# Second attention: scores of two heads to a block of 64 keys, in two TensorE tiles of 64 rows

## What is computed

```python
b, t1, _ = x.shape
q = x @ Wq + bq
kv = memory @ Wkv + bkv
k, v = jnp.split(kv, 2, axis=-1)
...
q_h = q_h * DK ** (-0.5)
scores = jnp.einsum('bhqd,bhkd->bhqk', q_h, k_h)
mask0 = memory_mask[:, None, :, :] == 0
scores = jnp.where(mask0, -jnp.inf, scores)
attn = jax.nn.softmax(scores, axis=-1)
attn = jnp.where(mask0, 0.0, attn)
ctx = jnp.einsum('bhqk,bhkd->bhqd', attn, v_h)
ctx = ctx.transpose(0, 2, 1, 3).reshape(b, t1, H * DK)
return ctx @ Wout + bout
```

## Time and profile before

| | us |
|---|---|
| median of 3 runs | 2684.61 |
| lowest, highest | 2684.14, 2685.75 |
| profiled execution | 2688.99 |
| its span in the trace | 2687.0 |
| TensorE busy | 2390.7 (89%) |
| VectorE busy | 1575.9 (59%) |
| ScalarE busy | 1234.0 (46%) |
| GpSimd busy | 696.5 (26%) |
| mean granted TensorE clock | 0.978 |

### The profile page before, as it was taken

One profiled execution on the slowest core, in us unless ns is written; L12 is line 12 of the kernel. 1 busy time (PEld: TensorE's weight loads), 2 busy tenths in 40 slices (PEclk: granted clock), 3 DMA queues, 4 the chain that ended last, 5 costly groups with the idle time before them and its releaser, 6 DMA issues.

```text
span 2687.0 us, 37065 instructions
## 1 busy us (share of the span) xinstructions
PE 2390.7 (89%) x13032; PEld 1320.1 (49%) x13032; DVE 1575.9 (59%) x3089; ACT 1234.0 (46%) x2842; POOL 696.5 (26%) x1001
## 2 busy tenths in 40 slices
PE   8889999988888999898888999998888899998776
PEld 3655444445465544354546554454555655444343
DVE  4664624468676561557867555065786746525687
ACT  5753211268584412128858331213876823121485
POOL 0002321037301232013720213102570021310265
PEclk9999999999999999999999999989999999999988
DMA  8001100010300200000030101101003010100000
GB/s 291 17 10 64 33 16 32 0 48 9 110 16 10 70 28 21 27 16 32 9 124 2 57 23 28 39 9 48 1 16 116 2 56 23 44 0 1 1 1 32
DMA packets 58988, 99.43 MB, mean 37 GB/s; under 512 B 13364, under 2 KB 13748, under 8 KB 58296
## 3 DMA queue, kind: packets, MB, share of 16 engines
q1 hardware_dynamic: 58808, 97.06, 10.8%
HBM read 88.66 MB, written 8.39 MB: 36 GB/s over the span
## 4 chain that ended last, share of the span: by engine, by line
PE 63%; ACT 15%; DVE 11%; issue 7%; POOL 3%; DMA 0%; ACTq 0%; DVEq 0%; POOLq 0%; SPq 0%
PE psum L379 21%; PE psum L373 17%; ACT prob L779 6%; PE psum L457 3%; PE psum L523 2%; PE psum L473 2%; ACT xT L808 2%; POOL f_y L362 2%; ACT f_a L966 2%; PE psum L760 1%; DVE f_top L1356 1%; PE psum L665 1%; PE psum L543 1%; PE psum L732 1%; PE psum L594 1%
## 5 line engine op out<-in xcount | busy, mean ns | idle before, releaser
L373 PE MATMUL psum<-xT,weights 128*128 128x512 f32 x1152 | 508.5, 596 | 19.1 <-DMA weights<-in_a_k 10.4
L373 PEld LDWEIGHTS psum<-xT,weights 128*128 128x128 f32 x1152 | 215.1, 191 | 271.5 <-issue 253.2
L379 PE MATMUL psum<-weights,mixed 128*128 128x512 f32 x768 | 337.3, 595 | 3.1 <-DVE mixed L1302 3.1
L1067 DVE TENSOR_REDUCE neg_max<-psum 128x1 f32<-128x128 f32 (+3 forms) x512 | 217.6, 483 | 136.6 <-PE psum L466 71.2
L379 PE MATMUL psum<-weights,xT 128*128 128x512 f32 x640 | 288.9, 596 | 2.4 <-DVE recip L1259 1.6
L1394 POOL TENSOR_SCALAR var<-stats 128x1 f32<-128x1 f32 x192 | 61.7, 321 | 796.3 <-DVE stats L1012 796.3
L779 ACT ACTIVATE prob<-psum,neg_max 128x128 f32<-128x128 f32 (+3 forms) x512 | 263.1, 542 | 4.5 <-DVE neg_max L1067 4.4
L1407 POOL TENSOR_TENSOR f_a<-f_a,f_z 128x256 f32<-128x256 f32 x256 | 193.0, 759 | 166.9 <-DVE f_a L1074 163.9
L379 PEld LDWEIGHTS psum<-weights,mixed 128*128 128x128 f32 x768 | 143.4, 190 | 179.9 <-issue 173.3
L1042 DVE TENSOR_TENSOR x<-psum,x 128x512 f32<-128x512 f32 x128 | 88.4, 690 | 223.4 <-PE psum L379 161.4
L1074 DVE SCALAR_TENSOR_TENSOR f_a<-f_g,conv_w,f_a 128x256 f32<-128x256 f32 x256 | 173.1, 676 | 52.3 <-ACT f_a L966 51.6
(11 more groups left out here) (242 smaller groups left out, 4063.3 us busy)
## 6 DMA issues: line engine op xcount, KB each, us to landing
xT<-in_xT SPq DMA_DIRECT2D x8, 1024.0 KB, 6.6
x<-in_x SPq DMA_DIRECT2D x8, 1024.0 KB, 8.3
out<-x SPq DMA_DIRECT2D x16, 512.0 KB, 2.8
weights<-in_a_k SPq DMA_DIRECT2D x4, 1024.0 KB, 5.0
weights<-in_a_q SPq DMA_DIRECT2D x4, 1024.0 KB, 5.0
weights<-in_a_v SPq DMA_DIRECT2D x4, 1024.0 KB, 5.3
w1f<-in_w SPq DMA_DIRECT2D x4, 1024.0 KB, 14.8
w2f<-in_w SPq DMA_DIRECT2D x4, 1024.0 KB, 17.4
```

Of the source, the lines that this page charges most:

```text
L373: last = mm(bank[:, 0:n], weights[weight][:, c, heads(g)], rhs(c), start=(c == 0), stop=(c == C - 1))
L379: last = mm(bank, lhsT(c), weights[weight][:, c, :], start=(c == 0), stop=(stop and c == C - 1))
L1067: last = v.tensor_reduce(sb["neg_max"][:, n, qc, j:j + 1], bank[:, o:o + P * (qc + 1)], AX.X, ALU.max, negate=True)
```

## The change

A token tile's 16 heads are now scored in one step, in two banks. The step of the first half (`half == 0`) claims two banks, puts the mask in both, and for each chunk `g` runs two products side by side: the partitions 0 to 63 (heads 4g and 4g + 1) into the first bank, the partitions 64 to 127 (heads 4g + 2 and 4g + 3) into the second. Each has 64 rows of contraction and 128 columns, two heads of 64 keys. The step of the second half issues nothing on TensorE but its waits. `b_k` keeps 2 x 64 columns a chunk instead of 4 x 64, and a half now holds two heads of every chunk instead of four heads of two chunks; so the copy to `b_turned` and the sum to `b_sum` write the same elements in another order.

```diff
@@ TensorE, b_score
-                    bank = dve_ring.claim(pe, step)
-                    mm(bank, sb["row_ones"][:], sb["b_mask_row"][:], start=True, stop=False)
-                    for i in range(2):
-                        last = mm(bank[:, 256 * i:256 * i + 256], sb["b_q"][:, 2 * half + i, w * D + P * t:w * D + P * t + P],
-                                  sb["b_k"][:, 2 * half + i, :], start=False, stop=(i == 1))
-                    last.then_inc(dve_ring.filled, 1)
+                    if half == 0:
+                        pair = [dve_ring.claim(pe, ("b_score", w, t, a)) for a in range(2)]
+                        for bank in pair:
+                            mm(bank, sb["row_ones"][:], sb["b_mask_row"][:], start=True, stop=False)
+                        for g in range(C):
+                            for a, bank in enumerate(pair):
+                                r = slice(2 * HD * a, 2 * HD * a + 2 * HD)
+                                last = mm(bank[:, heads(g)], sb["b_q"][r, g, w * D + P * t:w * D + P * t + P],
+                                          sb["b_k"][r, g, :], start=False, stop=(g == C - 1))
+                                if g == C - 1:
+                                    last.then_inc(dve_ring.filled, 1)
@@ ScalarE, b_context
-                            last = run(sb["b_k"][r, g, SK * j:SK * j + SK], bank[r, 0:SK], ACT.Identity,
+                            last = run(sb["b_k"][r, g, SK * (j % 2):SK * (j % 2) + SK], bank[r, 0:SK], ACT.Identity,
                                        bias=sb["b_bias"][r, C + g:C + g + 1])
@@ ScalarE, b_turn
-                    copy(sb["b_turned"][:, w, 4 * half:4 * half + 4, heads(t)],
+                    copy(sb["b_turned"][:, w].rearrange("p (g a) n -> p g a n", a=2)[:, :, half, heads(t)],
                          act_ring.take(act, step).rearrange("p (k n) -> p k n", k=4)).then_inc(act_ring.freed, 1)
@@ VectorE, b_turn
-                    v.tensor_reduce(sb["b_sum"][:, 2 * half:2 * half + 2, t, :],
-                                    sb["b_prob"][:, i % HALF_SLOTS, :].rearrange("p (g j k) -> p g j k", g=2, j=G),
+                    v.tensor_reduce(sb["b_sum"][:, :, t, 2 * half:2 * half + 2],
+                                    sb["b_prob"][:, i % HALF_SLOTS, :].rearrange("p (g j k) -> p g j k", g=C, j=2),
                                     AX.X, ALU.add).then_inc(q["b_summed"], 1)
@@ place
-    again(room, room2, ("b_k", [C, G * SK]), ("b_v", [2 * C, 64]), ("b_q", [C, S]), ("b_prob", [HALF_SLOTS, D]),
+    again(room, room2, ("b_k", [C, 2 * SK]), ("b_v", [2 * C, 64]), ("b_q", [C, S]), ("b_prob", [HALF_SLOTS, D]),
```

## The result

The changed kernel takes 2689.19 us (median of 20 runs, 2687.52 to 2692.3), the kernel before 2685.02 in the runs beside it (20 runs, 2683.84 to 2686.63). Ratio 1.0016, interval 1.0009 to 1.0023: 4.2 us slower, where 7.6 faster was forecast. It lies above the forecast range of 2670 to 2687.5. The profiled execution took 2689.32 (span 2687.3). That is only 0.3 us more span than the kernel before has in its profile (2687.0), whose execution lay 4 us above its median; so whole runs are compared by medians here, and the profiles are used for single stages.

The account below looks back on a forecast made before the run. TensorE was taken as most of the chain of waits, with VectorE setting the pace in places. From 2689.0 us profiled, 6.0 for the stage and 1.6 for the clock gave 2681.4, or 2677.0 off the median; range 2670 to 2687.5.

Parts of the forecast that it names:

- The score step, 1.66: Token tile's whole score step on TensorE: 1.66 us instead of 2.16, saving 0.50 eight times an element.
- The rival that the tiles do not run side by side: Score step's two 64-row tiles do not overlap: 2.46 us instead of 1.66, whole kernel at 2701 us; chance 9%.
- The new wait of 1.7 at the start: Stage start: the second pair waits for VectorE to free a bank, so TensorE stands 1.7 us.
- Then TensorE is again the late one: Behind the start wait TensorE sets the pace: fifth pair done at 924.35, first row step 0.34 us earlier.
- R to O0, 12.85: From the first row step to the first output tile: 12.85 us, where it was 14.05.
- The wait of 0.8 for `mixed`: First output tile: a new TensorE wait of 0.8 us, as the last value result passes VectorE behind half 14.
- Behind O0 nothing differs: After the first output tile, turns and output tiles stay bound by TensorE, with no change in time.
- The gain of 1.5 an element: Stage start to first output tile 1.5 us shorter in each of four elements, 6.0 us in all.
- The smaller edits, priced at nothing: Halved `b_k` zeroing, turned copy and sum with other strides, second semaphore increment: no time counted.
- VectorE keeps the stage: Dearer tile entry and exit (step 1.75 to 1.95 us) let bank waits eat the gain: mid 2684 us; chance 24%.
- The clock, one fall of three saved: Shorter wait before the row step spares one of three falls to the 0.50 clock, 1.6 us.
- The rival that the clock falls more often: The 1.7 us wait at each stage start brings a clock fall in all four elements: 2685 us; chance 5%.

Follow-up runs that it names:

- late query wait: Changed kernel with the wait for each `b_q` copy asked behind the mask passes, just ahead of the product needing that group: 2684.65 us, ratio 1.0002.
- new order: First window's steps reordered so TensorE's requests were made to other engines steps earlier: kernel before 2669.75 us (0.9947), changed kernel 2652.14 us (0.9882).
- row later: Changed kernel with the second row step moved from ahead of the turn of half 9 to behind the first value step: 2679.90 us, ratio 0.9978.
- filled at rows: Changed kernel with 8 idle mask passes ahead of the wait for the first row step only, in every element: 2684.27 us, ratio 0.9997.
- filled kernel before: Kernel before with 11 idle mask passes ahead of the wait for the first row step of every element: 2684.60 us, ratio 0.9996.
- pairs without tiles: Kernel before with both halves of a token tile scored in one step claiming two banks, old full-row products, no tiles: 2686.76 us, ratio 1.0010.
- both repairs: Changed kernel with `b_q` copies waited for group by group and the second row step behind the first value step: 2674.08 us, ratio 0.9961.
- shifted: Changed kernel with 8 idle mask passes (1.73 us) once, ahead of the first element's first score step: 2689.83 us, ratio 1.0017.
- filled at pair: Changed kernel with 6 idle mask passes ahead of the second pair's claim of banks, in each element: 2689.62 us, ratio 1.0018.

## Why the prediction was wrong

- **The score step, 1.66.** Right: 1.61. The rival that the tiles do not run side by side (9%) is out.
- **The new wait of 1.7 at the start.** Right: 1.59. That it brings no low clock was right as well.
- **"Then TensorE is again the late one", fifth pair done at 924.35, R 0.34 earlier.** Failed: the fifth pair was done 26.80 us behind the stage's start (896.34 to 923.14) instead of 26.38, and R came 0.01 earlier. The sum had TensorE's work only and left out ScalarE. Before, the scores of half 7 and a turn stood between the last projection and half 8; now only the turn does, and the fifth pair asks for the whole of `b_q` ahead of its mask passes. The late query wait measured 0.52 for it.
- **R to O0, 12.85.** Failed: 13.57. I took the sixth pair out from behind R and went on with T and V without asking for the bank. Before, the scores of half 11 between R and T gave ScalarE the time for turn 8's copy. Moving the row step measured 0.93 for it, and gave 12.64. The wait of 0.8 for `mixed` was there with 0.51.
- **Behind O0 nothing differs.** Off by 0.10 an element.
- **The gain of 1.5 an element.** 0.39 was there. With both waits repaired it is 84.38 - 82.54 = 1.84, so these two waits are enough to account for what was missing.
- **The smaller edits, priced at nothing.** Right: the sum takes 0.676 us and the turned copy 0.568, in both kernels within 0.001.
- **VectorE keeps the stage (24%).** Its time, 2684, was nearest but one, and its mechanism is not what happened: the score step had its forecast length, and ScalarE's copies ended the waits that ate the gain. The rule of the Trainium skill weighed there (TensorEngine Tiling, Performance Considerations, PSUM Bottleneck), that the emptying of PSUM may become the bound, fits the two ScalarE waits in kind; the new order shows that it is a matter of when they are asked for, and no bound of the engine.
- **The clock, one fall of three saved.** Failed, with the wrong sign. I looked at the length of the wait ahead of R (down to 1.70) and not at what else stands beside it. With the wait for `b_turned` close behind R, TensorE was busy 1.70 and then 2.75 of 3.41 us (fourth element), and a second low stretch followed in two of the three elements that were hit. With either wait away no element of the profiles has low clock behind R: row later takes out the second, filled at rows fills the first. In the medians this is the larger part: filling the wait at R alone gives back 4.9 us. The rival that the clock falls more often (5%, 2685) was nearest in outcome and named the wrong wait.

The sum in the terms of the prediction: 6.0 of gain was 1.6 (4.4 short), and 1.6 from the clock became a loss of 5.8 (1.6 + 4.2). The 5.8 is what the medians leave, not a reading. The profiled executions show 2.1 of it in stage B: what S to O0 has above its clean value, 7.0 against 4.9. Stage D may hold more. There a wait of 2.17 us for `d_thin` is followed by low clock in one element and not in another of the same execution. The kernel before, first and second element:

```profile
431.23 0.31 PE L621 MATMUL psum<-flow_eps,d_thin 128*32 128x2 f32 x16 [2.16 <-DVE d_thin L1051]
431.38 1.04 PE L391 MATMUL psum<-d_qT,d_thin 128*32 128x512 f32 x8
432.35 0.66 PE L613 MATMUL psum<-ident,d_kT 128*128 128x128 f32 x4
...
1087.95 0.31 PE L621 MATMUL psum<-flow_eps,d_thin 128*32 128x2 f32 x16 [2.17 <-DVE d_thin L1051]
1088.10 1.04 PE L391 MATMUL psum<-d_qT,d_thin 128*32 128x512 f32 x8
1089.08 0.89 PE L613 MATMUL psum<-ident,d_kT 128*128 128x128 f32 x4
1089.90 1.94 PE L391 MATMUL psum<-d_kT,d_thin 128*32 128x512 f32 x8
```

From stage C to the first product with `d_halves` it is 115.7 us without and 117.28 with the low clock. The kernel before has it in one element and the changed kernel in three, 3.1 us more. With the 2.1 that is near the 5.8, but it is not shown to be the rest: from the first product with `d_halves` on to the next stage B, or the last product, the same two executions differ by 3.5 us the other way (1626.9 us before, 1623.4 changed, four elements together), and that is why their spans are only 0.3 apart. The filled kernel before has it in four elements, so against the 4.9 that filling gave in stage B stand 4.7 in stage D. That would fit its 0.7, but that execution too differs behind stage D, by 4.0. How the loss outside stage B is made up, and why a given element is hit, stays open; I made no experiment on stage D, and these are single executions.

## What to carry to other kernels

- When a step is made shorter or taken out from between two others, list for each step behind it everything it asks for: the bank, the copy on the third engine, and where that copy stands in that engine's own order. The two waits here show as 0.34 and 0.67 us and took 1.45 of the 1.84 us an element that the change had to give.
- Price a cheaper step by what the stage still waits for: in the old order 4.3 us of TensorE's work saved brought 1.3 over pairs without tiles; in an order nearly without waits the whole change brought 3.8 over the kernel before in that order. Change the order and the step together.
- Look for two waits close to each other with little work between them: here they went with a lower clock, which cost more than the idle time. Moving the second away gained 9.3 us, of which 3.7 was its own.

## What was not expected of the hardware

- A wait of 1.70 us ahead of the row step had no low clock behind it when work without a gap followed (row later, both repairs: none in four elements), and had 1.4 to 2.9 us of loss behind it in three elements of four when a second wait of 0.67 stood 1.9 us later. Over the four kernels that keep both waits (changed, shifted, filled at pair, late query wait) 9 of 16 elements have low clock behind R; over the two without the second wait none of 8, over the two with the first one filled none of 8, and with 1.02 and 0.66 (pairs without tiles) none of 4.
- A longer wait does not mean more loss: with 2.50 ahead of R one stretch of 3.41 us at 0.50 followed (loss 1.63), with 1.70 and 0.67 two of them (loss 2.7 and 2.85).
- Two tiles of 64 rows cost no more at the entry and exit than was read from four tiles of 32: a whole step 1.61, with 1.09 for the 16 passes and the way out.
